# Maximum products of the cross attentions over 64 rows, two heads at a time

## The reference

```python
def _L1_xattn_ref(hidden_states, encoder_hidden_states, Wq, Wk, Wv, Wo, bo):
    ...
    scores = jnp.einsum('bhsd,bhkd->bhsk', q, k) * scale
    probs = jax.nn.softmax(scores, axis=-1)
    out = jnp.einsum('bhsk,bhkd->bhsd', probs, v)
    out = out.transpose(0, 2, 1, 3).reshape(B, S, H * Dh)
    out = out @ Wo + bo
    return out
```

## Time and profile before

| | us |
|---|---|
| three runs | 468.27, 469.48, 469.94 |
| median | 469.48 |
| profiled execution, span from first to last instruction | 466.1 |
| median of the runs above that span | 3.4 |
| TensorE busy | 370.9 (80%) |
| VectorE busy | 299.3 (64%) |
| ScalarE busy | 201.6 (43%) |
| GpSimd busy | 120.9 (26%) |
| heads of cross0 and cross1 | about 87 to 95, 317 to 323 |
| steady part of cross0, of cross1 | 94.6 to 147, 322.8 to 433 |

### The profile page before, as it was taken

One profiled execution on the slowest core, in us unless ns is written; L12 is line 12 of the kernel. 1 busy time (PEld: TensorE's weight loads), 2 busy tenths in 40 slices (PEclk: granted clock), 3 DMA queues, 4 the chain that ended last, 5 costly groups with the idle time before them and its releaser, 6 DMA issues.

```text
span 466.1 us, 6364 instructions
## 1 busy us (share of the span) xinstructions
PE 370.9 (80%) x2210; PEld 183.2 (39%) x2210; DVE 299.3 (64%) x688; ACT 201.6 (43%) x381; POOL 120.9 (26%) x105
## 2 busy tenths in 40 slices
PE   2588878789998688888888844287999999999635
PEld 2223324244465332333435510143444455446514
DVE  4487834657734645767743899547777876763475
ACT  1255553355462521454443721023555566555141
POOL 8100000045672000000000124101546545568012
PEclk9999998999999765899797865569999999999866
DMA  8923110003000200320200000000032312300000
GB/s 209 225 62 75 30 40 0 24 1 80 12 2 25 67 0 0 87 51 3 66 3 1 2 1 0 0 0 23 13 80 69 80 26 67 81 0 1 1 1 23
DMA packets 18127, 17.85 MB, mean 38 GB/s; under 512 B 5424, under 2 KB 12336, under 8 KB 18096
## 3 DMA queue, kind: packets, MB, share of 16 engines
q1 hardware_dynamic: 18096, 17.45, 15.7%
HBM read 6.11 MB, written 0.26 MB: 14 GB/s over the span
## 4 chain that ended last, share of the span: by engine, by line
PE 59%; DVE 27%; ACT 5%; issue 4%; DMA 2%; SPq 1%; POOL 1%; DVEq 0%; POOLq 0%
PE ACC L645 10%; PE PS L616 9%; DVE mx L1126 6%; PE PS L525 6%; PE PS L537 4%; PE PS L520 4%; DVE mx L1128 3%; PE PS L510 3%; PE ACC L663 3%; PE PS L522 2%; PE PS L581 2%; DVE V L1365 2%; PE PS L729 2%; PE ACC L638 2%; PE PS L610 2%
## 5 line engine op out<-in xcount | busy, mean ns | idle before, releaser
L960 ACT ACTIVATE Pr<-PS 128x512 f32<-128x512 f32 x160 | 90.8, 590 | 62.5 <-PE PS L616 33.8
L473 POOL TENSOR_TENSOR Psum<-Pr 128x512 f32<-128x512 f32 x24 | 31.2, 1300 | 133.6 <-ACT Pr L960 133.0
L1128 DVE TENSOR_REDUCE mx<-PS 128x1 f32<-128x512 f32 x96 | 60.0, 681 | 6.9 <-PE PS L537 6.9
L616 PE MATMUL PS<-Q,K 128*128 128x256 f16 x384 | 56.0, 273 | 1.3 <-DMA Q<-mrow 1.3
L645 PE MATMUL ACC<-Pr,V 128*64 128x256 f32 x384 | 55.9, 396 | 0.0
L616 PEld LDWEIGHTS PS<-Q,K 128*128 128x128 f16 x384 | 34.6, 98 | 25.7 <-issue 16.0
L1126 DVE TENSOR_REDUCE mx<-PS 128x2 f32<-128x512 f32 x64 | 39.6, 682 | 2.2 <-PE PS L534 2.0
L475 POOL TENSOR_TENSOR Psum<-Psum,Pr 128x512 f32<-128x512 f32 x24 | 30.4, 1267 | 39.0 <-ACT Pr L960 39.0
L537 PE MATMUL PS<-K,Q 128*128 128x512 f16 x96 | 34.8, 384 | 4.1 <-DVE mx L1128 2.0
L1192 DVE TENSOR_TENSOR Zs<-ACC,Zs 128x256 f32<-128x256 f32 x24 | 10.2, 425 | 43.3 <-ACT Zs L976 43.3
L534 PE MATMUL PS<-Kr,Q 128*128 128x256 f16 x128 | 25.6, 294 | 10.7 <-DVE Q L1157 4.6
(11 more groups left out here) (250 smaller groups left out, 582.5 us busy)
## 6 DMA issues: line engine op xcount, KB each, us to landing
K<-Kh SPq DMA_DIRECT2D x48, 128.0 KB, 2.3
K<-Kl SPq DMA_DIRECT2D x24, 128.0 KB, 2.3
Q<-Ql SPq DMA_DIRECT2D x24, 64.0 KB, 2.0
Q<-mrow SPq DMA_DIRECT2D x44, 1.0 KB, 1.7
wq_c<-in_c_Wq_dram SPq DMA_DIRECT2D x1, 512.0 KB, 8.8
wo_c<-in_c_Wo_dram SPq DMA_DIRECT2D x1, 512.0 KB, 10.5
Pr<-in_ctx_dram SPq DMA_DIRECT2D x1, 384.0 KB, 3.8
wk_c<-in_c_Wk_dram SPq DMA_DIRECT2D x1, 384.0 KB, 7.4
```

The costliest lines, as they stand in the source:

```text
L473: alone(nc.gpsimd.tensor_tensor(t, p[:, 0, :], p[:, 1, :], ALU.add), "sums_done")
L616: last = mm(dst[:, h * S:(h + 1) * S], K_[:, u % 3, h, keys], Q_[:, u % 3, h, b * S:(b + 1) * S], start=(first == 0), stop=(first == 1))
L960: A(Pr[:, n % 3, half * 512:(half + 1) * 512], SC3[:, m % 3, :], ACT.Exp, scale=ph.scale).then_inc(sem("exp_done"), 1)
L1128: last = v.tensor_reduce(mx[:, u % 2, t, i % 2:i % 2 + 1], src, AX, ALU.max)
```

## The change

Three edits. The maximum product reads only the 64 rows of the head's own side, so that it computes K high times Q high; head 0 lies on rows 0 to 63 and head 1 on rows 64 to 127. After a job in a slot TensorE takes the next one at once if it is a `max` with odd i, so that the two heads of one query tile are issued one behind the other, into two AUX banks. And in slot 0 the K projection is planned ahead of all four `max` jobs, where it stood behind the first.

```diff
@@ -129,7 +129,7 @@
             elif u < U:
-                jobs = [mx(u + 1, 0, 1) + (one("k", u + 2, 1) if u >= 1 else []) + mx(u + 1, 1, 4),
+                jobs = [(one("k", u + 2, 1) if u >= 1 else []) + mx(u + 1, 0, 4),
                         mx(u + 1, 4, 8), one("turn", u + 1, 2) + one("q", u + 2), one("k", u + 3)][c]
@@ -534,8 +534,9 @@
                     else:
-                        last = mm(dst, Q1[:, u % 3, i % 2, t * P:(t + 1) * P],
-                                  K1[:, u % 3, i % 2, b * SC:(b + 1) * SC], start=True, stop=True)
+                        own = slice(64 * (i % 2), 64 * (i % 2) + 64)
+                        last = mm(dst, Q1[own, u % 3, i % 2, t * P:(t + 1) * P],
+                                  K1[own, u % 3, i % 2, b * SC:(b + 1) * SC], start=True, stop=True)
@@ -689,6 +690,8 @@
                         if jobs:
                             aux(jobs.pop(0))
+                            if jobs and not ph.small and jobs[0][1] == "max" and jobs[0][3] % 2 == 1:
+                                aux(jobs.pop(0))
```

## The result

| | before | after |
|---|---|---|
| median | 468.88 us (4 runs) | 475.26 us (473.57 to 477.01, 4 runs) |
| ratio, 95% interval | | 1.012 (1.0074 to 1.0166) |
| profiled execution, own time | not kept apart | 476.5 us |
| its span | 466.1 us | 474.8 us |

The changed kernel is 1.2% slower, some 5.6 us by the ratio, whose interval reaches from 3.5 to 7.8 us. The two medians lie 6.4 us apart; what follows goes by the ratio. I had forecast slower, by 2.3 us; the median lies just above the top of my range (475.0). A later set of runs of the same two kernels gave 1.0103 (1.0062 to 1.0143), about 4.9 us.

A forecast was written before the change was run, and what follows sets the result against it. TensorE fills the windows, but VectorE's fixed list and three banks bound the half unit. Six full units +1.3 and two others +1.1 give +2.3 us (rounded): span 466.1 to 468.4, plus 3.4, 471.8 us; range 469.0 to 475.0.

The forecast's parts named there:

- The half unit: Chunks 0 and 1 of a full unit: waits of 1.17 us against savings of 0.96, so 7.99 us instead of 7.78.
- Product 2: Maximum product in chunk 0: waits 0.26 us for VectorE's K low half to free its bank, starting at 3.01.
- the second pair: Maximum products 4 and 5 in chunk 1, side by side, starting 5.06 us after the unit's start.
- product 6: Maximum product in chunk 1 at 5.92 us; its partner waits 0.31 for product 4's reduce, starting at 6.23.
- the units without a K projection: Unit 2 of cross0, unit 6 of cross1: half unit from 7.27 to 7.81 us, +0.54 each, +1.1 together.
- product 3: In units without a chunk-0 K projection, this maximum product waits for VectorE's first reduce and starts at 3.01 us.
- Rival A: TensorE's saving comes through in 8 units, 0.96 us each: 7.7 us off, 461.8 us; chance 0.06.
- The 64-row switch: TensorE changing between 128-row and 64-row products: 0.10 us at each change, with about 0 as the other bound.
- Rivals B and C: B: free switches, about 0 in all, 469.4, chance 0.07; C: pairs run in sequence, +3.4 to +5.5, chance 0.12.
- The heads: Start of each cross phase, paced by VectorE: single products, switches of 0.10 us lie in TensorE's idle time, cost 0.
- my rival D: More TensorE pauses lower the granted clock in the phases; ten microseconds at half clock add up to 5; chance 0.03.
- Bank waits: Maximum products waiting for VectorE to free auxiliary banks: +1.3 us in six full units, +1.1 in two others, +2.3 rounded.

## Why the prediction was right, and where it was not

**The half unit.** The forecast for a full one was 7.99 us; measured 7.96 to 7.98 in six units. Product 2 was put at 3.01 (2.99 measured), its partner at 3.61 (3.59), the second value half at 3.93 (3.91), the second pair at 5.06 (5.03), product 6 at 5.92 (5.90), its partner at 6.23 (6.21), chunk 2 at 7.99 (7.97). For the units without a K projection 7.81 was forecast; cross1's took 7.81 us, product 3 starting at 3.00 where I had 3.01:

```profile
415.24 0.61 PE L617 MATMUL PS<-Q,K 128*128 128x256 f16 x4
416.04 0.39 PE L538 MATMUL PS<-K,Q 64*128 64x512 f16 x2 [0.19 <-DMA Q<-Ql]
...
416.90 0.39 PE L538 MATMUL PS<-K,Q 64*128 64x512 f16 x1
418.24 0.39 PE L538 MATMUL PS<-K,Q 64*128 64x512 f16 x1 [0.95 <-DVE mx L1131]
...
423.05 0.50 PE L617 MATMUL PS<-Q,K 128*128 128x256 f16 x3
```

What carried this was to stop reading TensorE's full windows as room for savings, and to follow the three banks piece by piece through VectorE's fixed list. Rival A (461.8 us) died of exactly that: the 0.96 us per unit were saved and given back as waits.

**The 64-row switch** was bounded by the 96-row projection (0) and one-row products (0.10); it is 0.10. (I had written that one-row products were the only ones on a part of the rows. Besides the 96-row projections the trace of the kernel before has sixteen products over 20 rows, L559, from 224.38 us on, which I did not use.) The Trainium skill's rule on a change of tiling mode (TensorEngine Tiling (Array Packing), Key Properties) agrees. So does its statement that products on distinct row groups run together (TensorE: Matmul & The Clock Gate, Part 3: Packing small matmuls): the pairs that met free banks lie within the length of one product, which I had taken from pairs on distinct columns. Rivals B and C fell with that.

**The heads** were the term that failed. I put them and the units 0 behind them at nothing, by the sentence that a switch lies in idle time. That sentence held as far as the switch goes; what it left out is the clock, my rival D, to which I gave 0.03: "In the head it stayed 1.00 with TensorE busy 60%; little chance." I read a clock of 1.00 in a head of 128-row products as a margin that 64-row products would keep too. I also took all eight for single products, where the first two run side by side. The runs showed the lower level in both heads instead, at a price of 3.1 us by the stages: 1.05 in the heads and 2.0 in the units 0 behind them, where the scores ran at the lower level until 100.5 and 332.6 us. Between the second profiles of the two kernels it is 2.75 us (0.85 and 1.90). So what had a chance of 0.03 became the larger half of the loss.

**The sum.** Bank waits 2.3 forecast; by stages 1.14 for the six units and 1.1 for the other two (0.54 and 0.55, the 0.78 without a releaser left out): 2.2. Clock 3.1. Together 5.3, against 5.6 and 4.9 from the two ratios. The way was right; the size was short by the clock's term.

## What to carry to other kernels

A stretch in which the bottleneck engine is 100% busy can still have no room: list what the pieces there hand on, by which buffers, and when the reader of each buffer gets to it. Where a ring of three buffers feeds an engine that is full in just that stretch, pairs of pieces belong where the buffers are free, and saving TensorE time on them comes second. And when an edit makes matmuls smaller, look for the sparsest stage that contains them and ask what the granted clock does there, and what runs right behind it.

## What the runs showed of the hardware that I had not expected

The granted clock fell from 2.4 to 1.2 GHz in the heads, some fourteen products each, when eight of them were reduced from 128 to 64 rows, though each took as long (0.39 us) and, in the first profile, the pauses before the fall were the same but for one, 0.57 us instead of 0.35; in cross1 the same products, issued twice, kept it up. The fall came 0.6 to 3.9 us after a head's first product, and its cost mostly in the dense unit behind the head. A second point: parts of the program that no kernel of this study touches differ by 4 to 6 us from one profile to another (the first product starts at 87.9 to 92.2 us, the stretch from cross0's last scores to cross1's first product takes 174.4 to 180.2), so a comparison of two single profiles must be made stage by stage.
